# Local attention on one core: another order of the work on PE, DVE, ACT and POOL

## The reference

```python
h = shift_token(x)                       # half of the channels one token later
q, k, v = jnp.split(h @ wqkv, 3, axis=-1)    # 8 heads of 64
q = l2norm(q) * qs
k = l2norm(k) * ksc
q, k = rotary_xpos(q, k)                 # q * cos + rotate_half(q) * sin, scaled by place
o = local_attention(q, k, v)             # windows of 64, each sees itself and the one before
x = x + o @ wo
# then layer norm, gated unit (GELU), and a second layer of the same
```

## Time and profile before

| | |
|---|---|
| median of 3 runs | 1972.62 us (1968.84 to 1976.2) |
| profiled execution | 1974.57 us, span 1972.8 us |
| busy in the span | PE 89%, ACT 75%, DVE 56%, PEld 53%, POOL 22% |
| granted TensorE clock, mean | 0.959 |
| local attention, first layer | about 1100 to 1432 us of the span |
| local attention, second layer | about 1537 to 1870 us |
| L1149, the products of norm | 128 of 1231 ns on average, 157.5 us |
| L1139, L873, L883, L892 in the whole run | see the rows below |

### The profile page before, as it was taken

One profiled execution on the slowest core, in us unless ns is written; L12 is line 12 of the kernel. 1 busy time (PEld: TensorE's weight loads), 2 busy tenths in 40 slices (PEclk: granted clock), 3 DMA queues, 4 the chain that ended last, 5 costly groups with the idle time before them and its releaser, 6 DMA issues. The chain is left out here.

```text
span 1972.8 us, 68063 instructions
## 1 busy us (share of the span) xinstructions
PE 1765.5 (89%) x28076; PEld 1051.8 (53%) x28076; DVE 1112.6 (56%) x3304; ACT 1487.9 (75%) x2649; POOL 425.4 (22%) x351
## 2 busy tenths in 40 slices
PE   8888899999999999999998788888879688888888
PEld 5664555555555555555554355555633355555533
DVE  5444533333333333333311699999853698989754
ACT  3333699999998999999998478887833587877733
POOL 1004000000000000000000556565300665565200
PEclk9988999999998999999999899998999899999999
DMA  1000311111111111111101201010000010010000
GB/s 56 3 3 24 113 51 53 59 46 58 50 56 42 58 58 58 59 58 46 42 16 55 57 18 25 16 23 14 17 1 0 20 25 18 18 23 13 18 11 32
DMA packets 42339, 69.60 MB, mean 35 GB/s; under 512 B 7377, under 2 KB 33105, under 8 KB 42065
## 3 DMA queue, kind: packets, MB, share of 16 engines
q1 hardware_dynamic: 42064, 65.66, 10.6%
HBM read 21.08 MB, written 2.10 MB: 12 GB/s over the span
## 5 line engine op out<-in xcount | busy, mean ns | idle before, releaser
L653 ACT ACTIVATE x_probs<-x_pss 128x1024 f32<-128x1024 f32 x832 | 806.4, 1021 | 51.7 <-PE x_pss L574 35.5
L588 PE MATMUL x_acc<-x_probs,x_v 128*32 128x256 f32 x6656 | 437.9, 380 | 0.1
L574 PE MATMUL x_pss<-x_qx,x_kx 32*128 32x256 bf16 x9984 | 348.4, 270 | 14.1 <-issue 6.3
L574 PEld LDWEIGHTS x_pss<-x_qx,x_kx 32*128 32x128 bf16 x9984 | 221.4, 93 | 199.8 <-ACT x_probs L653 180.3
L588 PEld LDWEIGHTS x_acc<-x_probs,x_v 128*32 128x32 f32 x6656 | 206.6, 110 | 93.5 <-issue 9.4
L1245 ACT ACTIVATE l_prob<-l_sim,l_neg_top,l_inv_norm 128x128 f32<-128x128 f32 x512 | 245.3, 485 | 0.4
L700 DVE COPY x_vnext<-x_psp 128x128 f32<-128x128 f32 (+1 forms) x199 | 59.1, 297 | 315.4 <-PE x_psp L552 312.3
L873 POOL TENSOR_TENSOR l_turned_half<-l_raw,l_tabB 128x512 f32<-128x512 f32 x128 | 160.2, 1272 | 155.7 <-ACT l_raw L1197 155.7
L629 POOL COPY x_zq<-zT 128x256 f32 (+1 forms) x15 | 6.0, 401 | 763.6 <-PE x_psp L559 695.4
L1149 DVE TENSOR_TENSOR l_prob<-l_prob,l_inv_total 128x512 f32<-128x512 f32 x128 | 157.5, 1231 | 4.4
L883 POOL TENSOR_TENSOR l_direct<-l_direct,l_turned_half 128x1024 f32<-128x1024 f32 x64 | 150.8, 2356 | 0.0
(11 more groups left out here) (172 smaller groups left out, 2826.7 us busy)
## 6 DMA issues: line engine op xcount, KB each, us to landing
x_kx<-x_kp SPq DMA_DIRECT2D x96, 208.0 KB, 2.3
x_cT<-in_context SPq DMA_DIRECT2D x16, 832.0 KB, 4.5
x_qx<-x_qp SPq DMA_DIRECT2D x48, 192.0 KB, 3.1
l_vmid<-l_vt SPq DMA_DIRECT2D x64, 128.0 KB, 2.3
xT<-in_x SPq DMA_DIRECT2D x8, 256.0 KB, 5.2
shifted<-zT SPq DMA_DIRECT2D x32, 64.0 KB, 2.0
out_x<-xT SPq DMA_DIRECT2D x8, 256.0 KB, 2.0
shifted<-zT SPq DMA_DIRECT2D x32, 63.8 KB, 2.0
```

The source lines that it names most:

```text
L574: ins = pe.matmul(pss[bank(k, 2 * p + r // 2)][:, r % 2, e, :], kx[par][rows, g, j * P:(j + 1) * P], qx[par][rows, g, a * S:(a + 1) * S], ...
L588: ins = pe.matmul(acc[32 * r:32 * r + 32, 0:S], v[:, j, g, r, :], probs[SLOT[p]][r // 2][:, r % 2, e, :], start=(u == 0), stop=(u == UNITS ...
L653: act.activation(probs[SLOT[p]][y][:, :, :, :], pss[bank(k, 2 * p + y)][:, :, :, :], ACT.Sigmoid, scale=HD ** -0.5).then_inc(weighed, 1)
```

## The change

Only `local_attention` changes, and in it only the order of the steps in the four functions `turn`, and what the order needs in waits. Some steps pass from one turn to its neighbour (project_v(x,0) stands at the end of the turn before, as do copy_v, the first mask, place_queries and a copy; on POOL, turn_halves(x+2,1) and join(x+2,0) pass to the next turn's start). PE's wait for the mask of the first two halves of scores moves from project_q to turn_over. `turn_halves` gets a wait for `joined`, which the new order needs since the join that last read that half of turned_half now stands right before it.

```diff
--- before.py
+++ after.py
@@ -869,6 +869,7 @@
                     n, r, _ = x
                     pool.wait_ge(raw_q, 2 * n + t + 1)
                     pool.wait_ge(raw_k, 2 * n + t + 1)
+                    at_least(pool, joined, 2 * n + t - 1)
                     for lo, frm in ((0, FD // 2), (FD // 2, 0)):
                         pool.tensor_tensor(heads(turned_half[t][:, :, lo:lo + FD // 2]),
                                            heads(raw[t][:, :, frm:frm + FD // 2]),
@@ -894,21 +895,19 @@
                                        ALU.mult).then_inc(scaled[t], 1)
 
             def turn(x):
+                turn_halves(later(x, 1), 1)
+                join(later(x, 1), 0)
+                turn_halves(later(x, 2), 0)
                 scale_keys(later(x, 1), 0)
-                turn_halves(later(x, 2), 0)
                 join(later(x, 1), 1)
                 scale_keys(later(x, 1), 1)
-                turn_halves(later(x, 2), 1)
-                join(later(x, 2), 0)
 
             pool.wait_ge(ready, 2)
             turns(pool, turn)
 
         @block.tensor
         def _(pe):
-            def project_q(x, t, scores_of=None):
-                if scores_of and exists(scores_of):
-                    pe.wait_ge(masked, 4 * scores_of[0] + 2)
+            def project_q(x, t):
                 if exists(x):
                     n, r, q = x
                     if t == 0:
@@ -994,7 +993,9 @@
                                                 kT[r % 2][rows, p, lo:hi], start=True, stop=True)
                     ins.then_inc(scored, 1)
 
-            def turn_over(x, b, h):
+            def turn_over(x, b, h, scores_of=None):
+                if scores_of and exists(scores_of):
+                    pe.wait_ge(masked, 4 * scores_of[0] + 2)
                 if exists(x):
                     n, r, _ = x
                     pe.wait_ge(normed, 4 * n + 2 * b + h + 1)
@@ -1035,25 +1036,25 @@
                     ins.then_inc(out_ready, 1)
 
             def turn(x):
-                project_v(x, 0)
                 score(x, 0)
-                turn_over(later(x, -1), 0, 1)
+                project_q(later(x, 2), 0)
                 project_k(later(x, 2), 0)
-                project_q(later(x, 2), 0)
+                project_v(x, 1)
+                turn_over(later(x, -1), 1, 0)
+                project_q(later(x, 2), 1)
                 value(later(x, -1), 0)
-                turn_over(later(x, -1), 1, 0)
-                project_k(later(x, 2), 1)
-                turn_over(later(x, -1), 1, 1)
-                project_v(x, 1)
-                project_q(later(x, 2), 1, x)
+                turn_over(later(x, -1), 1, 1, x)
                 score(x, 1)
                 value(later(x, -1), 1)
                 flip_q(later(x, 1), 0)
+                turn_over(x, 0, 0)
+                project_k(later(x, 2), 1)
+                project_out(later(x, -1))
                 flip_k(later(x, 1), 0)
-                turn_over(x, 0, 0)
-                project_out(later(x, -1))
                 flip_q(later(x, 1), 1)
+                turn_over(x, 0, 1)
                 flip_k(later(x, 1), 1)
+                project_v(later(x, 1), 0)
 
             turns(pe, turn)
 
@@ -1157,27 +1158,27 @@
                     dve.tensor_tensor(zT[:, at], psvy[:, 0:S], zT[:, at], ALU.add).then_inc(added, 1)
 
             def turn(x):
-                sums(later(x, 1), 1)
-                copy_v(x, 0)
-                mask(x, 0, 0)
+                norm(later(x, -1), 1, 1)
+                multiply_q(later(x, 2), 0)
+                multiply_k(later(x, 2), 0)
+                copy_v(x, 1)
+                mask(x, 0, 1)
                 floor_of(later(x, 1))
-                norm(later(x, -1), 1, 0)
-                norm(later(x, -1), 1, 1)
-                multiply_k(later(x, 2), 0)
-                inverse_norms(later(x, 1))
-                mask(x, 0, 1)
-                multiply_q(later(x, 2), 0)
-                sums(later(x, 2), 0)
-                copy_v(x, 1)
                 norm(x, 0, 0)
                 multiply_q(later(x, 2), 1)
+                inverse_norms(later(x, 1))
+                mask(x, 1, 0)
+                sums(later(x, 2), 0)
+                mask(x, 1, 1)
                 multiply_k(later(x, 2), 1)
-                mask(x, 1, 0)
-                mask(x, 1, 1)
+                norm(x, 0, 1)
                 place_keys(later(x, 1), 0)
                 add(later(x, -1))
-                norm(x, 0, 1)
+                norm(x, 1, 0)
                 place_keys(later(x, 1), 1)
+                sums(later(x, 2), 1)
+                copy_v(later(x, 1), 0)
+                mask(later(x, 1), 0, 0)
 
             for tab, const, scales in ((tabA, "cosine", "scales"), (tabB, "sine", "scales_turned")):
                 dve.tensor_tensor(tab[:, :, :, :].rearrange("p t m d -> p t (m d)"),
@@ -1255,25 +1256,25 @@
                     act.activation(probT[b][:, HALF * h:HALF * h + HALF, :], pst[h][:, :, :], ACT.Copy).then_inc(copied, 1)
 
             def turn(x):
-                place_queries(x, 0)
-                squares(later(x, 1), 1)
-                copy(later(x, -1), 0, 0)
-                exps(later(x, -1), 1, 0)
-                place_queries(x, 1)
                 exps(later(x, -1), 1, 1)
                 copy(later(x, -1), 0, 1)
+                copy_q(later(x, 2), 0)
                 copy_k(later(x, 2), 0)
+                exps(x, 0, 0)
+                squares(later(x, 2), 0)
+                copy_q(later(x, 2), 1)
+                copy(later(x, -1), 1, 0)
                 roots(later(x, 1))
-                copy_q(later(x, 2), 0)
-                squares(later(x, 2), 0)
-                exps(x, 0, 0)
                 copy_out(later(x, -1), 0)
-                copy_k(later(x, 2), 1)
-                copy(later(x, -1), 1, 0)
                 copy(later(x, -1), 1, 1)
-                copy_q(later(x, 2), 1)
                 exps(x, 0, 1)
                 copy_out(later(x, -1), 1)
+                copy_k(later(x, 2), 1)
+                place_queries(later(x, 1), 0)
+                exps(x, 1, 0)
+                squares(later(x, 2), 1)
+                copy(x, 0, 0)
+                place_queries(later(x, 1), 1)
 
             act.preload_act_table_set("natural_log_exp_and_others")
             turns(act, turn)
```

## The result

The changed kernel takes 1892.66 us (median of 3 runs, 1890.89 to 1899.57) against 1972.62: a ratio of 0.960, interval 0.956 to 0.965. The forecast was 1897. Its profiled execution takes 1899.57 us (span 1897.5, mean granted clock 0.972 where before had 0.959), 75.0 less than the 1974.57 of before's.

A forecast was written before the change was run, and what follows sets the result against it. DVE was taken to bound the kernel, losing 3.8 us of each 20.06 us local-attention turn to collisions with POOL. New turns of 17.0 us save 26 x 3.0 = 78 us: 1974.6 - 78 = 1897 us, range 1870 to 1935.

The forecast's parts named there:

- DVE sets the turn and loses 3.8 us of it to POOL: Local attention: DVE's queue bounds each 20.06 us turn; its two-input products and POOL instructions exclude each other, costing 3.8 us.
- The two halves: Step-by-step walk of the new turn, cut at score(x+1,0): inverse norms to score, then score to the next inverse norms.
- Second half: From score(x+1,0) to the next inverse norms: 8.73 us of DVE work from place_keys' end, 0.13 before the score.
- First half: From the inverse norms to score(x+1,0): score starts at 7.62 or 8.77 us, depending on when norm(x,1,0)'s product runs.
- a miss: norm(x,1,0)'s product, offered at 6.28 us, waits for POOL's second turn_halves instruction until 7.43; the turn takes 17.4 us.
- a slip: norm(x,1,0)'s product runs between POOL's two turn_halves instructions and ends at 6.89 us; the turn takes 16.2 us.
- A slip and a miss, mixed two to one: 17.0 us: Mean turn forecast: two turns in three have norm(x,1,0)'s product wait for POOL's second turn_halves instruction, giving 17.0 us.
- 26 turns x 3.0 = 78 us: Total gain: 13 turns a layer each save 3.0 us; short end turns at zero, bound 5 us a layer.
- Rival (b): A new wait, PE's score chain at half clock, replaces the collisions: turns 17.6 to 19.6 us, 1931 us; chance 0.25.
- Rival (d): Slower: PE becomes the bound, with four tenths of its 15.9 us work at half clock; 2031 us, chance 0.03.
- (a): norm(x,1,0)'s product nearly always runs between POOL's two turn_halves instructions: 16.3 us a turn, 1877 us; chance 0.17.
- The signs: Expected in the new profile: L1149's product some 950 ns, L1139's under 250, clock 0.95 or above; place_keys waiting means wrong.

## Why the prediction was right, and where its sizes were off

- **DVE sets the turn and loses 3.8 us of it to POOL.** Right: taking POOL's length away took 3.5 us off the turn, and shorter pieces of the same work 2.8. The clock alone gave 5 us of the whole.
- **The two halves.** The walk's time 0 lies 0.1 us ahead of POOL's scaling, from which the trace is read here, so 0.1 is taken off or added. Second half, from score to the next scaling: 8.70 walked, 8.75 measured (1254.98 to 1263.73). First half: 8.67 walked for a miss, 8.85 measured; 7.52 for a slip, 7.69 to 7.84 measured. The product was offered at 6.18 in the walk and at 6.15 to 6.27 in the trace; that this spread lies across the edge was not walked, since PE's key transposes were left out of it.
- **A slip and a miss, mixed two to one: 17.0 us.** The mean of the first layer, 17.03, agrees, and both of its terms were off. The mix was 5 misses to 7 slips. A turn that slips in takes 16.6 us and not 16.2: PE waits up to 0.5 us for ACT's copy of the queries (l_qT) ahead of the score, a wait that I had left out. A miss takes 17.6 and not 17.4. Two errors of about 0.3 us a turn, the mix and the lengths, cancelled: the agreement of the mean is luck.
- **26 turns x 3.0 = 78 us**, against 75.0 between the two profiled executions. The second layer gained 25.0 us in twelve turns, 11 less than the first. What failed is the step that took the two layers as alike: DVE's 2.85 us stops at the loop's branches. Before shows such stops at the same two places, 1.20 and 1.94 us, and I had read no timeline there. The twenty-four turns gave 60.7 us where 72 were reckoned. What made up for it is what lies outside them, 14.3 us where I had set 6 for the thirteenth turns and nothing, with a bound of 5 a layer, for the ramps. That the total agrees is luck in this part too.
- **Rival (b), half clock after a wait ahead of the score.** Its mechanism is real, but only behind the stops: 3.54 us idle, then 0.50. Ahead of the score PE waits at most 1.43 us and the stretch's clock is 1.00, as the 1.21 us wait of before let me expect. **Rival (d)** fell with it: PE needs 187.72 / 12 = 15.6 us a turn at full clock. **(a)** needed the product offered 0.1 us sooner in 5 turns of 12.
- **The signs.** Products of L1150 844 and 890 ns (layer 2) for some 950; L1140 232 and 261 for under 250; one product a turn stretched by 1.06 us in the turns that miss, and the one before it by 0.1 to 0.3 in every turn; the clock 1.00 and 0.98; ACT at 16.0 us a turn. The sign of being wrong that did come is the wait of place_keys for PE's key transposes, told above. The moved wait of PE's turn_over cost nothing to be seen, where I had set 0.3 us of idleness (turn_over at 1261.30, right behind the matmuls that end at 1261.23).

What stays open: how much of the reordering each engine's queue contributes. Orders mixed from the old and the new queues were not tried on the chip.

## What to carry to other kernels

Where a DVE instruction that reads two SBUF tiles stands beside GpSimd work, compare the two timelines before moving anything. A longest duration that is the median plus about a GpSimd instruction's length was a collision here, and shorter GpSimd instructions were worth as much as a new order of four queues. How far to split has to be measured: pieces of 128x256 won another 29 us in the old order (1926 to 1897) and gained nothing in the new one (1893 to 1908), where every piece costs GpSimd time and meets another product. A schedule that clears a long instruction by a tenth of a microsecond is not clear of it: leave room, or see to it that the wait after a miss is short.

## What the runs showed of the hardware

The exclusion between the two engines goes by whole instructions and by who comes first, to within a tenth of a microsecond. With the join starting at 1247.13, a small product at 1247.02 took 0.17 us; with the join at 1258.31, one at 1258.39 took 2.29. And it lets DVE in between two GpSimd instructions that stand back to back: the product offered at 1219.00 took 0.69 us and GpSimd's second half waited for it. The Trainium skill (SBUF — State Buffer, "SBUF: two separate sides") describes the exclusion; these rows agree with it.

DVE's stop at the loop's branch back was 2.85 us in the second layer and 0.4 us in the first, for the same steps, and gone with the loop written out; a stop of 0.15 us at another fixed place of the program showed there. That it is the supply of instructions I only infer from this; why the layers differ no run shows.
